# A two-layer attention kernel: unread TensorE passes in the last second layer, ten small loads on another queue, units and jobs at other slots

## The chip, the cores and the metric

The kernel runs on 1 core of one Trainium2 chip. The metric is the device time of one execution, in microseconds (us); lower is better. The kernel before takes 3834.04 us, the median of 3 runs (3832.09 to 3839.49). The profiled execution is another one and took 3831.53 us.

## The reference, cut to what matters

For 64 sequences of 128 rows and 160 columns, and a context of 77 rows of 256 each:

```python
# layer 0, 20 heads of 64
n = layer_norm(x);  x = x + attention(n, n)          # self attention
n = layer_norm(x);  x = x + attention(n, context)    # cross attention
x = geglu_ff(layer_norm(x)) + x                      # 160 -> 2*640 -> 160
# layer 1, 20 heads of 8; 73 text rows and 4 image rows of the context
probs_t = softmax(q @ k_t * scale);  text = probs_t @ v_t
qsem = l2norm(probs_t @ text_ehs)                    # per head
fused = q @ k_ip * scale + 0.5 * (qsem @ l2norm(ip_ehs))
image = (softmax(fused) * spatial_mask) @ v_ip
out = (text + image) @ W_out + b_out + x
```

All of it is in 32-bit floats.

## The kernel before, in words

Four sequences make a group; there are 16 groups. One list of **slots** sets the order of everything: `STEP` is 60 slots to a group, and slot numbers run on, so the last group's first layer ends at slot 959 and its second layer lies behind it. In each slot at most one **unit** begins: in layer 0 (`"l0"`) one pair of heads of two sequences, 40 units to a group; in layer 1 (`"l1"`) four heads of one sequence, 20 units to a group. The second layer of group g is worked off between the first-layer units of group g+1: `L1_SLOT` lists its 20 slots, the first-layer units take those left. The last group's second layer has no first layer beside it; `LAST_L1_SLOT` lists its slots, 964 to 973 and 980 to 989.

Every engine walks through the slots in its own loop and does what each slot holds in a fixed order, so each engine's instructions are a fixed list, and only semaphores tie the engines together. A unit goes through five steps: scores on TensorE into a bank `PS` (`scores`, one slot ahead), maximum on VectorE (`softmax_in`), exponentials on ScalarE (`exp`), transposes on TensorE into `PT` (`probs_transposed`, a slot later), product with the values into a bank `PV` (`probs_v`, two slots later). For a first-layer unit VectorE also sums and GpSimd normalises (`prob_sums`, `normalise`), and `wo` adds its part of the output into the bank `PW`. For a second-layer unit VectorE does six instructions on the result, three slots after the unit's own (`unit_out`).

The other work is a **job** at a slot of its own: `qk`, `kc`, `v` (projections of a unit), `xT` (transposes after a layer norm), `ff` and `down`, `q1` and `k1` (second-layer queries and keys), `vip`, `ctx1` (per sequence b: Gram matrix and values of the context, copied into `gv`), and the tail of each sequence b of the second layer: `ipT`, `ip`, `oT1`, `y`. Jobs take the two banks `PG` in turn: a job waits until the last but one job's bank has been read. A layer norm (g, k, h), with h the half of the group, has its slot in `NORM_SLOT`; k = 0 to 2 are those of layer 0, k = 3 only copies rows.

Second-layer queries and keys reach their places by DMA, from SyncE's queue: three transfers for each of five parts w, `q1st` for each half and `k1st` for each group. GpSimd forms `kbd` from `k1st`.

Ahead of the loops stands a setup block (lines 242 to 310), which ends for all engines together. In it SyncE starts the loads of the first x and of the weights of keys, queries and values, ScalarE those of twelve small rows (`EARLY`: six of the layer norms, four biases, `b_1` and `fside`; `b_1` is read with 4 bytes to a piece). Then `SPLITS` are worked off at `SPLIT_SLOT`: each weight is split into a high part (ScalarE, `split_high`) and a low part (VectorE, `split_low`). The first group begins at slot -15, its first unit is at slot 20.

Of the kernel before, what the change touches and what calls it, by code (L numbers as in the profile page):

```python
# [5 lines left out]
def xattn_program(nc: bass.Bass, D, out: bass.AP):  # L6
# [13 lines left out]
    GROUPS = B // GB  # L20
    NP = H // 2
    HB = GB // 2
    HT = HB * 128
# [14 lines left out]
    F = FF // 128  # L38
# [4 lines left out]
    STEP = 60  # L43
    L1_SLOT = [6, 7, 9, 10, 11, 13, 14, 15, 17, 18, 22, 26, 27, 29, 33, 37, 41, 45, 49, 53]
    LAST_L1_SLOT = list(range(4, 14)) + list(range(20, 30))
    L0_SLOT = [s for s in range(STEP) if s not in L1_SLOT]
    NORM_SLOT = {(0, 0): -12, (0, 1): -2, (1, 0): 25, (1, 1): 40, (2, 0): 52, (2, 1): 65, (3, 0): 60, (3, 1): 71}
    FF_SLOT = [56, 56, 56, 56, 56, 68, 68, 68, 68, 68]
# [3 lines left out]

    SPLIT_SLOT = [8, 9, 17, 18, 28, 30, 31, 31, 32, 32, 49, 50]
    SPLIT_LOAD = [None, None, None, None, 21, 28, 21, 21, 21, 21, 47, 47]
    RAW_LOAD = {"kc": 22, "vc": 34}
    KEYS_ZERO = 32
    LEAD = {"q": 2, "kc": 1, "vc": 1}
    PLAIN_SLOT = 48

    FIRST_L0_SLOT = list(range(STEP - NL0, STEP))  # L60
    FIRST_NORM_SLOT = {(0, 0): 8, (0, 1): 22, (1, 0): 33, (1, 1): 43, (2, 0): 53}
    VIP_SLOT = 58
    K1_SLOT = (52, 58)

    PT_LAG, PV_LAG, OUT_LAG = 1, 2, 3
    CTX1_SLOT = {0: 59, 1: 65, 2: 82, 3: 89}
    LAST_CTX1_SLOT = {0: 58, 1: 65, 2: 80, 3: 85}

    ctx = ExitStack()
    with ctx:  # L70
# [171 lines left out]
        with nc.Block() as block:  # L242
            @block.sync
            def _(sp):
                sp.dma_start(xres[:, 0, :, :], x_dram[0:HB].rearrange("b n c -> n b c")).then_inc(x_first, 16)
                for i in range(2):
                    for src, p0, p1 in SPLITS[i][0]:
                        sp.dma_start(SPLITS[i][3][p0:p1], src).then_inc(split_in[i], 16)
                w = D["L0_xattn_a1_wq"]
                sp.dma_start(q_raw[:, 0, :], w[0:128, :]).then_inc(raw_in["q"], 16)  # L250
                for src, p0, p1 in rest_of(w):
                    sp.dma_start(q_raw[p0:p1, 1, :], src).then_inc(raw_in["q"], 16)
                for i in range(2, 4):
                    for src, p0, p1 in SPLITS[i][0]:
                        sp.dma_start(SPLITS[i][3][p0:p1], src).then_inc(split_in[i], 16)

            @block.scalar
            def _(act):

                for i, (dst, src) in enumerate(EARLY):  # L260
                    act.dma_start(dst, src, allow_slow_non_contiguous=True).then_inc(ln_in if i < 2 else early_in, 16)

# [102 lines left out]
        def slots(at):  # L365
            table = {}
            for t, what in at:
                table.setdefault(t, []).append(what)
            return lambda t: table.get(t, [])
# [3 lines left out]

        NORMS = sorted((STEP * g + (s if g else FIRST_NORM_SLOT.get((k, h), s)), g, k, h)
                       for g in range(GROUPS) for (k, h), s in NORM_SLOT.items())
        NORM = {x[1:]: i for i, x in enumerate(NORMS)}
# [12 lines left out]
        def ctx1_slot(g, b):  # L389
            return STEP * g + (CTX1_SLOT if g < GROUPS - 1 else LAST_CTX1_SLOT)[b]  # L390

        stacks_at = slots([(STEP * g + Q1_SLOT[h] + 1 + w, ("q1", g, h, w))
                           for g in range(GROUPS) for h in range(2) for w in range(W1)]
# [4 lines left out]
            + [(t + (1 if k == 3 else 2), ("xT", g, k, h)) for t, g, k, h in NORMS]  # L398
            + [(STEP * g + Q1_SLOT[h], ("q1", g, h)) for g in range(GROUPS) for h in range(2)]
            + [(STEP * g + PREP_SLOT[h] + 1, ("cT", g, h)) for g in range(GROUPS) for h in range(2)]  # L400
            + [(tail_slot(g, b) + d, (kind, g, b)) for d, kind in ((5, "ipT"), (6, "ip"), (7, "oT1"), (8, "y"))
               for g in range(GROUPS) for b in range(GB)]
            + [(STEP * g + FF_SLOT[F * h + F - 1] + 1, ("down", g, h)) for g in range(GROUPS) for h in range(2)]
            + [(STEP * g + s, ("ff", g, i)) for g in range(GROUPS) for i, s in enumerate(FF_SLOT)]
            + [(STEP * g + K1_SLOT[r], ("k1", g, r)) for g in range(GROUPS) for r in range(2)]
# [87 lines left out]
        with nc.Block() as block:  # L493
# [7 lines left out]
            def _(sp):  # L501
# [53 lines left out]
                def load_raw(kind):  # L555
                    sp.wait_ge(S["split_done"], 4 if kind == "kc" else 10)
                    w = D["L0_xattn_a2_wk" if kind == "kc" else "L0_xattn_a2_wv"]
                    for c, raw in enumerate(kc_raw if kind == "kc" else vc_raw):
                        sp.dma_start(raw, w[128 * c:128 * c + 128, :]).then_inc(raw_in[kind], 16)

                for t in range(FIRST, LAST):
                    for kind, i in stores_at(t):
                        store_slice(kind, i)
# [46 lines left out]
            def _(pe):  # L610
# [27 lines left out]
                def ctx_rows(ps, w, c0, n, b, rows):  # L638

                    for c in range(2):  # L640
                        for i, (hw, hc) in enumerate(SPLIT3):
                            last = mm(ps, cT[:, c, hc, TS * b:TS * b + rows], w[:, c, hw, c0:c0 + n],  # L642
                                      start=(c == 0 and i == 0), stop=(c == 1 and i == 2))
                    return last

                def slice_in(name):
# [197 lines left out]

                for t in range(FIRST, LAST):
                    if t + 1 in UNIT_AT:
                        scores(UNIT_AT[t + 1])
# [591 lines left out]
```

## Time and profile before

| | before |
|---|---|
| time, median of 3 runs | 3834.04 us |
| profiled execution | 3831.53 us |
| its span | 3829.7 us |
| TensorE busy (matmul) | 3622.5 us, 95% |
| VectorE busy | 2563.7 us, 67% |
| ScalarE busy | 2584.0 us, 67% |
| GpSimd busy | 1335.9 us, 35% |
| data moved by DMA | 313.38 MB, mean 82 GB/s |

The span runs from the first to the last instruction that the profiler saw; what lies around it is 1.8 us. Times in rows are counted from the span's start. The busy share of TensorE is an upper limit, since the ends of its pipelined matmuls are modelled. Its clock has two levels, 1.2 and 2.4 GHz; the granted clock is given as a share of the higher.

### The profile page before, as it was taken

To read this page: it belongs to the slowest core of one execution; us is meant where nothing else is said; L and a number is where in the kernel's file an instruction comes from. 1 tells how busy PE (TensorE), PEld (TensorE's weight loads), DVE (VectorE), ACT (ScalarE), POOL (GpSimd) and SP (SyncE) were. 2 spreads that over 40 slices of the span, in tenths; PEclk is the share of its full clock that TensorE was granted. 3 is DMA by queue.
4 is the path that set the end of the run, shared out by engine and by line. 5 is a ranking of instruction groups with operands and counts; after the bars stand their busy time and mean duration, and the time that the engine had idled before them with its cause. 6 is when DMAs were issued, how large, how long until landed. Compare 5 with 4: busy or idle time off the path is not lost. (4 is left out here: it accounts for less than half of the span.)

```text
span 3829.7 us, 88852 instructions
## 1 busy us (share of the span) xinstructions
PE 3622.5 (95%) x29632; PEld 3341.0 (87%) x29632; DVE 2563.7 (67%) x8159; ACT 2584.0 (67%) x8021; POOL 1335.9 (35%) x1658
## 2 busy tenths in 40 slices
PE   5999999999999999999999999999999999999988
PEld 5888989889898898989989898898988989899877
DVE  6667676676766767676676766767667676766755
ACT  5666676766767667676676767667676676766654
POOL 2233343333433334343333433334333343433323
PEclk9999999999999999999999999999999999999986
DMA  5522313223141322313223142231323223132220
GB/s 160 168 65 75 101 46 118 60 86 89 45 121 55 97 78 59 113 47 108 66 77 99 46 121 56 86 89 45 120 56 96 78 58 114 48 108 64 76 67 12
DMA packets 210716, 313.38 MB, mean 82 GB/s; under 512 B 31232, under 2 KB 167520, under 8 KB 210272
## 3 DMA queue, kind: packets, MB, share of 16 engines
q1 hardware_dynamic: 207392, 306.87, 27.2%
q8 instruction: 250, 4.10, 0.5%
q10 hardware_dynamic: 2880, 0.83, 0.1%
q14 instruction: 194, 1.59, 0.1%
HBM read 267.97 MB, written 14.42 MB: 74 GB/s over the span
## 5 line engine op out<-in xcount | busy, mean ns | idle before, releaser
L1376 POOL TENSOR_TENSOR SE<-SE,rs 128x512 f32<-128x512 f32 (+1 forms) x640 | 556.5, 870 | 1792.2 <-DVE rs L1210 1792.2
L961 ACT ACTIVATE SE<-PS,mx 128x128 f32<-128x128 f32 (+2 forms) x3840 | 979.0, 345 | 255.1 <-DVE qq L1234 109.1
L816 PE MATMUL PT<-ident,SE 128*128 128x128 f32 (+2 forms) x3840 | 585.9, 276 | 36.2 <-POOL SE L1376 35.3
L947 ACT ACTIVATE PTs<-PT 128x512 f32<-128x512 f32 (+2 forms) x960 | 574.7, 599 | 58.1 <-PE PT L816 38.7
L1205 DVE TENSOR_REDUCE sums<-SE 128x4 f32<-128x512 f32 (+1 forms) x640 | 366.8, 573 | 341.1 <-ACT SE L961 338.8
L1194 DVE TENSOR_REDUCE mx<-PS 128x4 f32<-128x512 f32 (+2 forms) x960 | 505.0, 526 | 59.4 <-PE PS L794 42.3
L816 PEld LDWEIGHTS PT<-ident,SE 128*128 128x128 f32 (+2 forms) x3840 | 469.9, 145 | 63.7 <-POOL SE L1376 49.6
L1368 POOL TENSOR_TENSOR n<-qq,p_half 128x4 f32<-128x4 f32 x320 | 323.0, 1009 | 469.1 <-DVE qq L1234 469.0
L774 PE MATMUL PW<-w_o,OTs 128*128 128x160 f32 x2560 | 417.0, 300 | 1.0 <-ACT OTs L939 1.0
L794 PE MATMUL PS<-qk 128*128 128x256 f32 x1280 | 348.9, 395 | 47.5 <-ACT qk L887 47.5
L884 ACT ACTIVATE qk<-PG 128x256 f32<-128x256 f32 x640 | 252.2, 394 | 196.1 <-PE PG L620 192.2
L830 PE MATMUL PV<-PTs,v_sb 128*64 128x128 f32 (+1 forms) x5120 | 370.9, 281 | 0.0
L774 PEld LDWEIGHTS PW<-w_o,OTs 128*128 128x128 f32 x2560 | 362.2, 191 | 1.4 <-ACT OTs L939 1.4
L840 PE MATMUL PV<-gv,PTs 73*128 73x86 f32 x2560 | 335.2, 275 | 0.7 <-DVE SE L1232 0.7
L830 PEld LDWEIGHTS PV<-PTs,v_sb 128*64 128x64 f32 (+1 forms) x5120 | 271.8, 137 | 67.2 <-issue 55.6
L840 PEld LDWEIGHTS PV<-gv,PTs 73*128 73x128 f32 x2560 | 325.1, 197 | 0.9 <-issue 0.8
L794 PEld LDWEIGHTS PS<-qk 128*128 128x128 f32 x1280 | 219.6, 191 | 101.5 <-issue 80.1
L617 PE MATMUL PG<-nT,q_slice 128*128 128x256 f32 x640 | 247.7, 387 | 28.2 <-DVE cipT L1108 10.6
L642 PE MATMUL PG<-vc_slice,cT 128*77 128x256 f32 x1920 | 265.5, 287 | 0.2 <-DVE nT L1115 0.2
L939 ACT ACTIVATE OTs<-PV 128x256 f32<-128x256 f32 x640 | 223.8, 381 | 57.0 <-PE PV L830 54.5
L1130 DVE COPY v_sb<-PG 128x512 f32<-128x512 f32 (+1 forms) x320 | 218.1, 682 | 57.5 <-PE PG L642 54.6
L887 ACT ACTIVATE qk<-PG 64x256 f32<-64x256 f32 x640 | 240.5, 376 | 3.7
(205 smaller groups left out, 7853.5 us busy)
## 6 DMA issues: line engine op xcount, KB each, us to landing
q_slice<-q_split SPq DMA_DIRECT2D x630, 192.0 KB, 2.5
vc_slice<-vc_split SPq DMA_DIRECT2D x155, 512.0 KB, 3.6
kc_slice<-kc_split SPq DMA_DIRECT2D x150, 256.0 KB, 2.7
q1st<-q_hi SPq DMA_DIRECT2D x320, 32.0 KB, 1.9
k1st<-k_hi SPq DMA_DIRECT2D x160, 38.5 KB, 1.9
xres<-in_x_dram SPq DMA_DIRECT2D x32, 160.0 KB, 2.3
q1st<-q_lo SPq DMA_DIRECT2D x160, 32.0 KB, 1.9
out_dram<-x SPq DMA_DIRECT2D x64, 80.0 KB, 1.6
```

Source lines behind the costliest of these rows:

```text
L642: last = mm(ps, cT[:, c, hc, TS * b:TS * b + rows], w[:, c, hw, c0:c0 + n], start=(c == 0 and i == 0), stop=(c == 1 and i == 2))
L774: last = mm(PW[:, C * b:C * b + C], OTs[:, n % 2, 128 * b:128 * b + 128], w_o[n // U0][:, p, :], start=(p == 0 and b == 0), stop=(p == NP ...
L794: last = mm(ps[:, 2 * J * b:2 * J * b + 2 * J], qk[:, n % 2, 0, 128 * b:128 * b + 128], keys[:, :, J * b:J * b + J], start=True, stop=True)
L816: last = tr(PT[0:J, 128 * i:128 * i + 128], SE[:, place % 4, J * i:J * i + J], ident[:, :])
L830: last = mm(PV[DH * e:DH * e + DH, 128 * b:128 * b + 128], v_sb[0:J, n // 2 % 2, b, 2 * (n % 2) + e, :], PTs[0:J, place % 3, 128 * i:128 * ...
L840: last = mm(PV[:, GV * i + off:GV * i + off + GS + D1], PTs[0:TT, place % 3, 128 * i:128 * i + 128], gv[:, b % 2, 2 * w + i // 2, off:off ...
L947: a_(PTs[0:J, place % 3, :], PT[0:J, :], ACT.Copy).then_inc(S["pts_done"], 1)
L961: last = a_(SE[:, place % 4, J * i:J * i + J], PS[place % 2][:, step * i:step * i + J], ACT.Exp, bias=mx[:, place % 2, i:i + 1])
L1194: v.tensor_reduce(mx[:, place % 2, :], sc[:, :, 0:J], AX, ALU.max, negate=True).then_inc(S["mx_done"], 1)
L1205: v.tensor_reduce(sums[:, n % 2, :], SE[:, place % 4, 0:4 * J].rearrange("p (i j) -> p i j", j=J), AX, ALU.add)\
L1368: gp.tensor_tensor(n20[:, b % 2, 4 * w:4 * w + 4], qq[:, b % 2, 4 * w:4 * w + 4], p_half[:, 0:4], ALU.pow)\
L1376: gp.tensor_tensor(e, e, rs[:, n % 2, :].unsqueeze(2).to_broadcast([128, 4, J]), ALU.mult)\
```

## The change

1. In the setup block ScalarE starts only the first two small loads. The other ten are started by SyncE at slot 10 (`EARLY_SLOT`). The five loads of the value weights move out of the setup block to the head of SyncE's loop. The split of `w_k0_rem` moves from slot 9 to 16.
2. Second-layer units 15 and 16 of every group but the last move from slots 37 and 41 to 36 and 38; five first-layer units move by a slot. `K1_SLOT` begins at 53 where it was 52.
3. For the last group alone: norm (2,1) from 65 to 63, (3,0) from 60 to 58, (3,1) from 71 to 69; the second half of `ff` from 68 to 67; `q1` from 62 and 73 to 61 and 72; `ctx1` from 58, 65, 85 to 59, 64, 84.
4. `keep_busy` is new: TensorE multiplies 128 x 128 by 128 x 256 of `nT` into `PW`, whose result nobody reads; 20 times ahead of the first scores of the last second layer, and 14 times ahead of each of its four `ipT`. That is 76 passes.

```diff
-    L1_SLOT = [6, 7, 9, 10, 11, 13, 14, 15, 17, 18, 22, 26, 27, 29, 33, 37, 41, 45, 49, 53]
+    L1_SLOT = [6, 7, 9, 10, 11, 13, 14, 15, 17, 18, 22, 26, 27, 29, 33, 36, 38, 45, 49, 53]
-    SPLIT_SLOT = [8, 9, 17, 18, 28, 30, 31, 31, 32, 32, 49, 50]
+    SPLIT_SLOT = [8, 16, 17, 18, 28, 30, 31, 31, 32, 32, 49, 50]
+    EARLY_SLOT = 10
...
-    LAST_CTX1_SLOT = {0: 58, 1: 65, 2: 80, 3: 85}
+    KEEP_BUSY = STEP * GROUPS + LAST_L1_SLOT[0] - 1
+    LAST_NORM_SLOT = {(2, 0): 52, (2, 1): 63, (3, 0): 58, (3, 1): 69}
+    LAST_FF_SLOT = [56, 56, 56, 56, 56, 67, 67, 67, 67, 67]
+    LAST_Q1_SLOT = [61, 72]
+    LAST_CTX1_SLOT = {0: 59, 1: 64, 2: 80, 3: 84}
...
-                for i in range(2, 4):
-                    for src, p0, p1 in SPLITS[i][0]:
-                        sp.dma_start(SPLITS[i][3][p0:p1], src).then_inc(split_in[i], 16)
...
-                for i, (dst, src) in enumerate(EARLY):
-                    act.dma_start(dst, src, allow_slow_non_contiguous=True).then_inc(ln_in if i < 2 else early_in, 16)
+                for dst, src in EARLY[0:2]:
+                    act.dma_start(dst, src, allow_slow_non_contiguous=True).then_inc(ln_in, 16)
...
+                for i in range(2, 4):
+                    for src, p0, p1 in SPLITS[i][0]:
+                        sp.dma_start(SPLITS[i][3][p0:p1], src).then_inc(split_in[i], 16)
                 for t in range(FIRST, LAST):
+                    if t == EARLY_SLOT:
+                        for dst, src in EARLY[2:]:
+                            sp.dma_start(dst, src, allow_slow_non_contiguous=True).then_inc(early_in, 16)
...
+                def keep_busy(n):
+                    pe.wait_ge(S["x_done"], 4 * GROUPS)
+                    for _ in range(n):
+                        mm(PW[:, 0:HT], nT[:, 0, 0, 0:128], nT[:, 0, 0, :], start=True, stop=True)
...
                 for t in range(FIRST, LAST):
+                    if t == KEEP_BUSY:
+                        keep_busy(20)
                     if t + 1 in UNIT_AT:
                         scores(UNIT_AT[t + 1])
...
                     for name in late_at(t):
+                        if name[0] == "ipT" and name[1] == GROUPS - 1:
+                            keep_busy(14)
```

SyncE's list at the start of the program, before (`SE`, `plain`, `kx1` and `later` hold raw weights; the branch at L242 is the end of the setup block):

```order
L245 DMA xres<-in_x_dram 128x2x160
L248 DMA SE<-in_L0_xattn_a1_wk_dram 128x1280
...
L252 DMA kx1<-in_L0_xattn_a1_wq_dram 32x1280 x4
L255 DMA later<-in_L0_xattn_a1_wv_dram 128x1280
L255 DMA later<-in_L0_xattn_a1_wv_dram 32x1280 x4
L242 UNCONDITIONAL_BRANCH
...
L573 DMA w_o0<-in_L0_xattn_a1_wo_dram 128x10x160
L519 DMA xres<-in_x_dram 128x2x160
...
L541 DMA q_split<-q_slice 128x384 x5
```

The same place after the change (the branch at L247 ends the setup block):

```order
L257 DMA kx1<-in_L0_xattn_a1_wq_dram 32x1280 x4
L247 UNCONDITIONAL_BRANCH
...
L574 DMA later<-in_L0_xattn_a1_wv_dram 32x1280 x4
L590 DMA w_o0<-in_L0_xattn_a1_wo_dram 128x10x160
L530 DMA xres<-in_x_dram 128x2x160
...
L578 DMA ln_g<-in_L0_xattn_ln2_g_dram 128x160
...
L578 DMA b_1<-in_L0_xattn_ff_b1_dram 128x10x1
L578 DMA fside<-in_fside_S_0_dram 128x1
L530 DMA xres<-in_x_dram 128x2x160
L552 DMA q_split<-q_slice 128x384 x5
```

The value weights now stand behind the end of the setup block, and the ten small loads behind them and ahead of the first stores of `q_split`.

VectorE's list in a middle group from slot 40 on, before (from the maximum of unit `l1` 16 on; `rr` to `qq` are `unit_out` of `l1` 15, `st6` the next layer norm):

```order
L1194 TENSOR_REDUCE mx<-PS1 128x4
L1199 COPY sip<-PS1 128x16
L1220 RECIPROCAL rr<-PV1 128x4
...
L1234 TENSOR_REDUCE qq<-SE 128x4
L1125 COPY kx1<-PG1 64x154 x2
L1130 COPY v_sb<-PG0 77x512
L1052 BN_STATS st6<-xres 128x6 x2
...
L1194 TENSOR_REDUCE mx<-PS0 128x4
L1125 COPY kx1<-PG0 64x154 x2
L1070 SCALAR_TENSOR_TENSOR nx<-lt,rstd,ln_b 128x128
```

The same place after the change (`rr` to `qq` are now `unit_out` of `l1` 16):

```order
L1222 TENSOR_REDUCE mx<-PS1 128x4
L1153 COPY kx1<-PG1 64x154 x2
L1080 BN_STATS st6<-xres 128x6 x2
...
L1233 TENSOR_REDUCE sums<-SE 128x4
L1238 RECIPROCAL rs<-sums 128x4
L1222 TENSOR_REDUCE mx<-PS0 128x4
L1248 RECIPROCAL rr<-PV0 128x4
...
L1262 TENSOR_REDUCE qq<-SE 128x4
L1153 COPY kx1<-PG1 64x154 x2
L1158 COPY v_sb<-PG0 77x512
L1098 SCALAR_TENSOR_TENSOR nx<-lt,rstd,ln_b 128x128
```

A `unit_out` that stood ahead of the norm's statistics has gone to the slot before, and the next one has come from slot 44 to 41, between the statistics and the norm's output.

TensorE's list at the end of the last first layer, before (from `vip` on):

```order
L734 MATMUL PG0<-plain,cipT 16x160 x2
L739 MATMUL PG1<-cT 73x82 x6
...
L744 MATMUL PG1<-vip_sb,pick 80x160
L816 MATMUL PT<-ident,SE 77x128 x4
...
L678 MATMUL PG0<-ident,nx 128x128 x4
L774 MATMUL PW<-w_o1,OTs 128x160 x4
L617 MATMUL PG1<-nT,w_q1h_hi 128x256
...
L620 MATMUL PG1<-nT,w_q1h_rem 128x256
L802 MATMUL PS0<-kbd,q1st 128x308
L747 MATMUL PG0<-ident,sip 80x128
```

And after the change:

```order
L758 MATMUL PG0<-plain,cipT 16x160 x2
L840 MATMUL PT<-ident,SE 77x128 x4
...
L702 MATMUL PG1<-ident,nx 128x128 x4
L763 MATMUL PG0<-cT 73x82 x6
...
L637 MATMUL PG1<-nT,w_q1h_rem 128x256
L798 MATMUL PW<-w_o1,OTs 128x160 x4
L668 MATMUL PW<-nT 128x256 x20
L826 MATMUL PS0<-kbd,q1st 128x308
L771 MATMUL PG0<-ident,sip 80x128
```

`ctx1` has gone behind the unit's transposes and products, `xT` and `q1` have come ahead of the last `wo`, and the 20 unread passes stand between that `wo` and the first scores.

## Rows read from the trace of the kernel before

**Rows 1.** Page: granted TensorE clock in 40 slices, in tenths

```profile
PEclk9999999999999999999999999999999999999986
```

**Rows 2.** Timeline of the setup: start us, length us, engine, line, what, idle before it

```profile
8.83 4.00 SPq L255 DMA_DIRECT2D later<-in_L_xattn_a_wv_dram  x5
9.76 9.45 ACTq L261 DMA_DIRECT2D fside<-in_fside_S_dram  x1
19.62 1.28 ACT L978 ACT_TABLE_LOAD   x1 [19.62 <-PEq L242]
```

**Rows 3.** Timeline of the first layer's start, same columns

```profile
24.80 3.56 DVE L1265 TENSOR_TENSOR w_k_rem<-plain,w_k_rem 32x1280 fp32r<-32x1280 f32 x2
...
25.40 1.60 POOL L1360 TENSOR_TENSOR xres<-xres,bias 128x320 f32<-128x320 f32 x1 [3.52 <-DMA fside<-in_fside_S_dram]
25.97 0.60 ACT L880 ACTIVATE nT<-PG 128x512 fp32r<-128x512 f32 x1 [2.62 <-PE PG L678]
...
30.32 0.55 PE L617 MATMUL PG<-nT,q_slice 128*128 128x256 f32 x1 [4.38 <-DVE q_slice L1277]
...
40.96 1.04 POOL L1376 TENSOR_TENSOR SE<-SE,rs 128x512 f32<-128x512 f32 x1 [13.96 <-DVE rs L1210]
```

**Rows 4.** Timeline of group 5 at slot 45, one of fifteen alike

```profile
1323.86 0.17 DVE L1220 RECIPROCAL rr<-PV 128x4 f32<-128x4 f32 x1
...
1324.81 0.46 DVE L1234 TENSOR_REDUCE qq<-SE 128x4 f32<-128x292 f32 x1
...
1325.87 0.39 PE L617 MATMUL PG<-nT,q_slice 128*128 128x256 f32 x1 [0.56 <-DVE kx L1125]
```

**Rows 5.** Windows of the last stretch: busy us (count) of each engine, then the granted clock

```profile
3711.00:3714.00 3.00, 2.00 (x12) 1.83 (x12) 2.49 (x8) 1.04 (x3) 2.10 (x3) 0.85 0.24 60
...
3759.00:3762.00 3.00, 2.42 (x21) 2.20 (x20) 2.89 (x15) 1.71 (x6) 1.21 (x2) 1.00 0.00 0
3783.00:3786.00 3.00, 3.00 (x15) 3.00 (x14) 2.30 (x11) 2.77 (x12) 0.70 (x1) 0.50 0.01 3
```

**Rows 6.** What TensorE waited for after 3700 us: total, times, longest

```profile
PE PG L747 <- DVE sip L1296: 9.1, 3, 3.9
...
PE PT L816 <- POOL SE L1376: 2.0, 1, 2.0
...
PE PW L774 <- ACT OTs L939: 1.0, 1, 1.0
```

**Rows 7.** Timeline where the last second layer starts, by engine

```profile
3723.10 0.69 DVE L1157 SCALAR_TENSOR_TENSOR q_lo<-PG,q_hi 128x512 fp32r<-128x512 f32 x1 [1.92 <-ACT q_hi L911]
...
3727.59 0.54 SPq L590 DMA_DIRECT2D q1st<-q_hi  x1
...
3726.97 0.59 PE L802 MATMUL PS<-kbd,q1st 96*128 96x308 f32 x1 [4.61 <-issue]
...
3730.78 0.60 PE L802 MATMUL PS<-kbd,q1st 96*128 96x308 f32 x1 [3.01 <-issue]
```

**Rows 8.** Chain that ended last: pieces on TensorE, at either clock

```profile
3720.86 0.21 PE PG L618
...
3754.35 0.44 PE PT L816 x4
3754.79 0.86 PE PV L840 x8
...
3790.79 0.26 PE PS L802
3791.05 0.85 PE PT L816 x4
3791.90 1.64 PE PV L840 x8
```

**Rows 9.** VectorE's timeline where it works without a gap

```profile
3758.86 0.45 DVE L1194 TENSOR_REDUCE mx<-PS 128x4 f32<-128x292 f32 x1
...
3760.63 0.45 DVE L1194 TENSOR_REDUCE mx<-PS 128x4 f32<-128x292 f32 x1
```

More of the change, by code:

```diff
@@ L43, in xattn_program @@
     STEP = 60
-    L1_SLOT = [6, 7, 9, 10, 11, 13, 14, 15, 17, 18, 22, 26, 27, 29, 33, 37, 41, 45, 49, 53]
-    LAST_L1_SLOT = list(range(4, 14)) + list(range(20, 30))
+    L1_SLOT = [6, 7, 9, 10, 11, 13, 14, 15, 17, 18, 22, 26, 27, 29, 33, 36, 38, 45, 49, 53]
+    LAST_L1_SLOT = [4, 5, 6, 7, 8, 9, 10, 11, 12, 13, 20, 21, 22, 23, 24, 25, 26, 27, 28, 29]
     L0_SLOT = [s for s in range(STEP) if s not in L1_SLOT]
@@ L62, in xattn_program @@
     VIP_SLOT = 58
-    K1_SLOT = (52, 58)
+    K1_SLOT = (53, 58)
     PT_LAG, PV_LAG, OUT_LAG = 1, 2, 3
     CTX1_SLOT = {0: 59, 1: 65, 2: 82, 3: 89}
-    LAST_CTX1_SLOT = {0: 58, 1: 65, 2: 80, 3: 85}
+    KEEP_BUSY = STEP * GROUPS + LAST_L1_SLOT[0] - 1
[3 more added lines that the diff above has]
+    LAST_CTX1_SLOT = {0: 59, 1: 64, 2: 80, 3: 84}
     ctx = ExitStack()
@@ L372, in xattn_program, with norm_slot, ff_slot, q1_slot @@
         outputs_at = slots((product_slot(UNIT_AT[t]) + OUT_LAG - PV_LAG, UNIT_AT[t]) for t in sorted(UNIT_AT))
-        NORMS = sorted((STEP * g + (s if g else FIRST_NORM_SLOT.get((k, h), s)), g, k, h)
-                       for g in range(GROUPS) for (k, h), s in NORM_SLOT.items())
+        def norm_slot(g, k, h):
+            own = FIRST_NORM_SLOT if g == 0 else LAST_NORM_SLOT if g == GROUPS - 1 else {}
+            return STEP * g + own.get((k, h), NORM_SLOT[(k, h)])
+        def ff_slot(g):
+            return FF_SLOT if g < GROUPS - 1 else LAST_FF_SLOT
+        def q1_slot(g):
+            return Q1_SLOT if g < GROUPS - 1 else LAST_Q1_SLOT
+        NORMS = sorted((norm_slot(g, k, h), g, k, h) for g in range(GROUPS) for k, h in NORM_SLOT)
         NORM = {x[1:]: i for i, x in enumerate(NORMS)}
@@ L390, in ctx1_slot @@
             return STEP * g + (CTX1_SLOT if g < GROUPS - 1 else LAST_CTX1_SLOT)[b]
-        stacks_at = slots([(STEP * g + Q1_SLOT[h] + 1 + w, ("q1", g, h, w))
+        stacks_at = slots([(STEP * g + q1_slot(g)[h] + 1 + w, ("q1", g, h, w))
                            for g in range(GROUPS) for h in range(2) for w in range(W1)]
@@ L398, in xattn_program @@
             + [(t + (1 if k == 3 else 2), ("xT", g, k, h)) for t, g, k, h in NORMS]
-            + [(STEP * g + Q1_SLOT[h], ("q1", g, h)) for g in range(GROUPS) for h in range(2)]
+            + [(STEP * g + q1_slot(g)[h], ("q1", g, h)) for g in range(GROUPS) for h in range(2)]
             + [(STEP * g + PREP_SLOT[h] + 1, ("cT", g, h)) for g in range(GROUPS) for h in range(2)]
@@ L402, in xattn_program @@
                for g in range(GROUPS) for b in range(GB)]
-            + [(STEP * g + FF_SLOT[F * h + F - 1] + 1, ("down", g, h)) for g in range(GROUPS) for h in range(2)]
-            + [(STEP * g + s, ("ff", g, i)) for g in range(GROUPS) for i, s in enumerate(FF_SLOT)]
+            + [(STEP * g + ff_slot(g)[F * h + F - 1] + 1, ("down", g, h)) for g in range(GROUPS) for h in range(2)]
+            + [(STEP * g + s, ("ff", g, i)) for g in range(GROUPS) for i, s in enumerate(ff_slot(g))]
             + [(STEP * g + K1_SLOT[r], ("k1", g, r)) for g in range(GROUPS) for r in range(2)]
```

## The prediction

> **What bounds the kernel now.** I read the page first. The granted clock [rows 1] is full nearly to the end and falls in the last two slices; TensorE is the only engine that is busy nearly throughout. So three places matter: the start, where it has no work yet; the fifteen middle groups, where a gain counts only if it removes a wait of TensorE; and the last second layer, where the clock is low.
>
> The timeline of the setup shows the start. SyncE has issued the query weights by 8.83 us and the value weights by 12.83, but the setup block ends at 19.6, because ScalarE's last small load holds its queue from 9.76 to 19.21 [rows 2]. Then a chain runs: layer norm, transposes, remainder split of `w_k0`, `nT`, `q_slice`, and the first projection at 30.32 [rows 3].
>
> A middle group, read by its timeline, has one TensorE wait that the moved units touch: 0.56 us at slot 45, where `qk` waits for a bank that VectorE's `kx` has not yet read, because a `unit_out` stands ahead of it [rows 4]. That `unit_out` lasts from 1323.86 to 1325.27, 1.41 us.
>
> The windows of the end show the clock falling at about 3713.1 (0.85 in that window of 3 us is 0.9 us at half), after TensorE had been busy for 2.00 of 3 us. It is full again for a time, at 2.42 busy of 3, and it is at half from 3783 on although TensorE is busy for 3.00 of 3 us with transposes and products of units [rows 5]. One unit's transposes and products then take 0.85 + 1.64 us against 0.44 + 0.86 at the full clock, and with its scores 2.75 [rows 8]. VectorE, without a gap, takes 1.77 us for a second-layer unit [rows 9]. So at 1.2 GHz TensorE sets the pace of this layer, and at 2.4 GHz VectorE does.
>
> **The change part by part.** The sum is made against the profiled execution, 3831.53 us; the median of the runs stands 2.5 above it, and I add the sum to the median.
>
> *Setup.* Without ScalarE's ten loads the block should end with SyncE's last issue, at 8.8, plus the same 0.4 us: 9.2 instead of 19.6, 10.4 earlier. Against that, the remainder split of 3.56 us has moved behind `nT`. It began at 24.80, and `nT` could have begun when ScalarE was done at 26.57 [rows 3]; the 1.8 us between were covered by the split and are a hole of VectorE now. 10.4 - 1.8 = 8.6, from which I take 0.6 for weights that land late: -8.0. The other end is a stall on SyncE's queue: its five value loads take 4.0 us, 0.8 each; four more loads and nine small ones at the same 0.8 would end at about 23.6; if `fside` then holds the queue for 9.45 us again, it is 33.1. Behind it stand the stores of `q_split`, which free the three `q_slice` buffers, and GpSimd's first normalisation stands behind `bias`, which waits for the same loads (they landed 15.6 us after `fside` was issued, at 25.40 [rows 3]; here at 39). Without the stall that normalisation is due at 40.96 - 8 = 33, so it would come about 6 us late: -2.
>
> *Units 15 and 16.* Work is unchanged. The 0.56 us goes, since no `unit_out` stands in slot 44 any longer. But VectorE now has `unit_out` of 15 at slot 39 and of 16 at 41, with the norm's statistics between them, and `kx` of slot 41 stands behind both, where TensorE's `qk` of slot 42 waits for its bank. By the listed order and the durations of this stretch VectorE comes there about half a us after TensorE. So a wait of 0.5 takes the place of 0.56: with a tenth for a smaller wait that goes too, 15 x -0.16 = -2.4. Bounds: the new wait is nothing, 15 x -0.66 = -9.9; or it is a whole `unit_out`, 15 x (1.41 - 0.56) = +12.7. `k1` a slot later is costed at nothing: TensorE has other work on both sides.
>
> *The last group up to the first second-layer scores.* `ctx1` no longer stands ahead of the last unit's exponentials, so the wait of 2.0 for GpSimd goes, and with `xT` and `q1` ahead of the last `wo` the wait of 1.0 for ScalarE [rows 6]. Then the clock need not fall at 3713.1: of the 9.2 us to the last pass of `q1` at 3722.36, 8.2 are busy and take half at 2.4 GHz, -4.1. The last `wo` is behind `q1` now: -0.5. Together -7.6, and the wait of 4.61 for `q1st` [rows 7] stays. Into it go the 20 unread passes. At 0.21 each at 1.2 GHz [rows 8] that is 4.2, at half of it 2.1; they start after the last `x` of VectorE, about 1 us after `q1` ends, so 2.1 is hidden and 4.2 would be late by about 0.6. Bounds: -3.5 (the clock falls as before) and -7.6.
>
> *From the first scores to the second half.* Part 1 of `q1st` stands behind a triple of `k1st`, as before, and part 2 now too: `q_lo` ends at 3723.79 and part 1 is issued at 3727.59, two triples later, 1.9 each [rows 7]. Against that `ctx1` of b = 1 goes into the wait, and `ff` is a slot earlier, which puts the dense passes ahead of a unit at the low clock (2.75 against 1.77, 1.0). I take -1, with 0 and -5 as bounds.
>
> *The 56 passes at the four `ipT`.* Three `ipT` have waited for VectorE's `sip`, 9.1 us in all, the longest 3.9 [rows 6]; there 14 passes take 2.9 or 1.5 us and are mostly hidden. The second stands in the middle of units with TensorE fully busy and costs 2.9 at 1.2 GHz. If the clock rises with it, each of the last eight units saves 2.75 - 1.77 = 0.98. I take half of this and the passes at half way between their prices: -3.9 + 2.2, and for jobs between the units -0.8: -2.5. Bounds: -7.3 (all eight, 1.5 for the passes, -1 for the jobs) and +2.9. In the last chain the two tails have their steps at half clock; if they run at the full one I count -2.6, if not, the passes that do not fit their gap cost +1.4. I take -1.
>
> Sum: -8.0 - 2.4 - 7.6 - 1 - 2.5 - 1 = **-22.5**: 3809.0 for the profiled execution, 3811.5 for the median.
>
> **The rivals.** *The clock holds.* If the dense passes keep the full clock through the last second layer, the four `ipT` parts give -7.3 and -2.6 instead of -2.5 and -1, and the first five units and `ff` some 3 us more: 9.4 more, 3802. Rows 5 speak against: TensorE busy 2.42 of 3 us was followed by a fall before 3783, and a share like it is what VectorE's pace leaves (0.44 + 0.86 of 1.77 us, and the scores). On what lets the clock fall, the Trainium skill, "TensorE: Matmul & The Clock Gate", section "Why this matters for your kernels", says that drops in mid-kernel are avoided by leaving no long idle gaps between matmul bursts. By that rule the clock would stay up between the second `ipT` and the end, and the time is this rival's, 3802. The trace does not bear it out, as the clock was at half with 3.00 of 3 us busy.
>
> *The start's gain is lost on SyncE's queue*: -2 instead of -8, 3817.5. For it speaks the 9.45 us of `fside`; against it that this was while all the first weights moved, and less is in flight at 24 us. The Trainium skill, "DMA: Bandwidth & Descriptors", section "Queues, rings and completion order", says that a DMA engine takes one queue's descriptors in order and takes turns between queues. By that rule the ten small loads, which had turns of their own on ScalarE's queue, now stand behind all the weights; the time is this rival's, 3817.5. No run shows it yet.
>
> *The passes don't do what they are for*: the clock is as before and they only cost: +2.9 and +1.4 instead of -2.5 and -1, 0 instead of -1, 8.8 more: 3820.
>
> *VectorE falls behind in every group.* Two `unit_out` within three slots delay the jobs behind them. If the new wait is one `unit_out`, the middle costs +12.7 and the sum is -7.4: 3826.6. If both are late, 2.8 us against 0.56, it costs 15 x 2.24 = +33.6, and the sum is +13.5: 3847.5, slower. It decides from a new wait of 1.9 us on (15 x 1.34 = 20.1, the rest of the sum). For it: VectorE is at work nearly without a gap there; against it: before, an even denser stretch of slots 40 and 41 was without a wait.
>
> **How the numbers follow.** Forecast 0.44, clock holds 0.18, start lost 0.15, passes only cost 0.09, one `unit_out` late 0.08, two late 0.06. A measurement of this kernel can tell some 0.2%, 7.7 us. Faster: the first four, 0.86; same: 0.08; slower: 0.06. The predicted time is the forecast's, 3811.5, rounded to 3811. Its own range, by the bounds of start and middle, is 3803 to 3822; the range reaches to the clock's rival with a middle wait gone (3802 - 7.5) and to one late `unit_out`: 3794 to 3826.
>
> **What would show it.** Setup block ends near 9.2, first projection near 22.3, the first `rs` of VectorE 8 us earlier. In a middle group no wait at slot 45 and one of about 0.5 at slot 42, the group 0 to 0.3 us shorter. First second-layer scores 7.6 us earlier against the last group's start, the clock full up to them, then half for some 10 us. Full clock after each block of 14, but not to the end. I am wrong if a group's length changes by over 0.5 us, if small loads land after the first normalisation is due, or if the clock holds.

## The result and the profile after

The changed kernel takes 3804.03 us, the median of 4 runs (3800.84 to 3805.68), where the kernel before takes 3834.81 in the same measurement (3832.09 to 3839.49). The ratio is 0.9928, 95% interval 0.9915 to 0.9941: 0.72% faster, some 28 us. The two medians of this measurement are 30.8 us apart; in the four later sets of runs the kernel before has medians of 3830.95 to 3832.64, which fits the 28. The forecast was 3811, the range 3794 to 3826. The profiled execution is the fastest of the four, 3800.84; its span is 3799.1, so the differences of the two traces below come to 30.6 us.

The page, in answer to [rows 1]:

```profile
PEclk9999999999999999999999999999999999999998
```

Windows of the last group cut at three scores of its second layer: start of the group to the first scores, to the eleventh, to the twentieth, to the end. Columns as in [rows 5]; the granted clock is the third number from the right. The kernel before:

```profile
3480.18:3726.97 246.79, 230.07 (x1878) 211.48 (x1877) 158.05 (x504) 161.40 (x501) 83.24 (x102) 0.97 0.23 66
3726.97:3777.95 50.98, 40.74 (x230) 38.41 (x231) 30.44 (x122) 22.96 (x66) 18.38 (x23) 0.67 0.07 18
3777.95:3805.79 27.84, 27.59 (x130) 26.02 (x131) 15.81 (x68) 14.01 (x47) 9.90 (x13) 0.51 0.06 15
3805.79:3829.71 23.92, 12.32 (x65) 9.14 (x64) 12.83 (x59) 5.18 (x17) 6.04 (x6) 0.63 0.03 8
```

And the changed kernel:

```profile
3470.55:3709.95 239.40, 229.10 (x1897) 210.77 (x1897) 156.78 (x504) 161.92 (x501) 84.48 (x102) 1.00 0.23 67
3709.95:3753.88 43.93, 34.27 (x246) 32.17 (x245) 29.69 (x122) 23.03 (x66) 18.37 (x23) 0.88 0.10 25
3753.88:3776.46 22.58, 21.11 (x144) 18.91 (x145) 15.35 (x67) 13.58 (x47) 9.91 (x13) 0.85 0.05 13
3776.46:3799.09 22.63, 14.29 (x91) 12.26 (x91) 13.07 (x60) 5.31 (x17) 6.05 (x6) 0.87 0.03 8
```

The four stretches are 7.4, 7.1, 5.3 and 1.3 us shorter. With the start (group 1 begins at 221.48 where it began at 226.14, 4.7) and fourteen groups that together take 3249.07 us and took 3254.04 (5.0), that is the whole difference. The prediction had 7.6, then 4.5 for the last three together (measured 13.6), 8.0 for the start and 2.4 for the groups. So what was new to explain is the gain behind the first scores, and whether the unread passes bring it. These are differences of two single executions; the experiments show that some 9 us of them lie with an early fall of the clock, which the kernel before has in some executions only, and some 4 with a stretch that no other execution repeats.

Timeline of the start, in answer to [rows 2] and [rows 3]:

```profile
8.71 1.28 ACT L1006 ACT_TABLE_LOAD   x1 [8.71 <-PEq L247]
...
11.44 8.83 SPq L530 DMA_DIRECT2D xres<-in_x_dram  x1
...
19.82 0.42 ACT L1019 ACTIVATE q_slice<-kx 128x256 fp32r<-128x256 f32 x1 [3.39 <-DMA kx<-in_L_xattn_a_wq_dram]
...
21.43 2.98 DVE L1293 TENSOR_TENSOR w_k_rem<-plain,w_k_rem 32x1280 fp32r<-32x1280 f32 x2 [0.27 <-ACT w_k_rem L1006]
...
24.66 0.55 PE L634 MATMUL PG<-nT,q_slice 128*128 128x256 f32 x1 [8.87 <-DVE w_k_rem L1293]
...
32.05 1.07 POOL L1388 TENSOR_TENSOR xres<-xres,bias 128x320 f32<-128x320 f32 x1 [21.08 <-DMA fside<-in_fside_S_dram]
...
35.68 1.04 POOL L1404 TENSOR_TENSOR SE<-SE,rs 128x512 f32<-128x512 f32 x1 [2.56 <-DVE rs L1238]
```

The setup block ends at 8.7, 10.9 us earlier, a little better than the 9.2 that was forecast. But the first projection comes at 24.66, only 5.7 earlier: ScalarE waits 3.39 us for the query weights to land, `w_k_rem` follows behind, and TensorE waits for it. The stall of 9.45 us that ScalarE's queue had is now one of 8.83 us on SyncE's queue, on the load of `xres`. The small loads land at 32.05. GpSimd then adds `bias`, is done at 33.12, and waits 2.56 us more: its first normalisation begins at 35.68 (40.96 before), released by VectorE's `rs`, not by `bias`.

A middle group, in answer to [rows 4]; first the kernel before at slots 52 and 53, which the prediction did not look at:

```profile
1352.05 0.42 ACT L918 ACTIVATE k_hi<-PG 128x292 fp32r<-128x292 f32 x1 [1.45 <-PE PG L730]
...
1353.50 0.43 ACT L884 ACTIVATE qk<-PG 128x256 f32<-128x256 f32 x1
...
1354.16 0.56 PEld L794 LDWEIGHTS PS<-kx,qk 128*128 128x128 f32 x4 [0.30 <-issue]
```

The changed kernel in the same places:

```profile
1346.27 1.19 PE L651 MATMUL PG<-cT,w_k1h 128*128 128x328 f32 x6
1346.38 0.40 ACT L912 ACTIVATE qk<-PG 128x256 f32<-128x256 f32 x1
...
1347.65 0.51 PE L818 MATMUL PS<-kx,qk 128*128 128x154 f32 x2
```

Before, `k1` was projected ahead of the unit's `qk`; its two copies `k_hi` stood ahead of the exponentials on ScalarE, `qk` was copied at 1353.50, and TensorE's scores waited 0.30 us for it. Now `k1` is projected while ScalarE copies `qk`. Slots 52 and 53 take 5.18 us where they took 5.52. The stretch of the moved units, slots 34 to 45, takes 44.53 and took 44.61.

### The profile page after: what moved, and what is told of

Same layout as the page of the kernel before. It is cut to its first block, busy times and chain, and to the rows that moved or that the text cites. A ratio compares the mean times of both kernels' runs of the same rounds, so it can differ in the third digit from the quotient of the medians.

```text
span 3799.1 us, 88944 instructions
## 1 busy us (share of the span) xinstructions
PE 3608.9 (95%) x29708; PEld 3328.8 (88%) x29708; DVE 2547.7 (67%) x8159; ACT 2592.4 (68%) x8021; POOL 1352.4 (36%) x1658
## 4 chain that ended last, share of the span: by engine, by line
PE 60%; DVE 17%; ACT 11%; issue 8%; POOL 4%; DMA 1%; SPq 0%; ACTq 0%; DVEq 0%; POOLq 0%
PE PS L818 8%; PE PT L840 6%; PE PV L854 6%; PE PW L798 5%; PE PG L659 5%; ACT SE L989 4%; PE PG L651 4%; PE PG L634 4%; PE PV L864 3%; DVE sums L1233 3%; PE PG L637 3%; PE PG L635 3%; PE PG L636 3%; POOL SE L1404 3%; PE PG L742 2%
## 5 line engine op out<-in xcount | busy, mean ns | idle before, releaser
L1396 POOL TENSOR_TENSOR n<-qq,p_half 128x4 f32<-128x4 f32 x320 | 345.3, 1079 | 490.2 <-DVE qq L1262 490.1
L864 PEld LDWEIGHTS PV<-gv,PTs 73*128 73x128 f32 x2560 | 317.5, 192 | 1.2 <-issue 1.1
```

The lines of the kernel that those rows point to most:

```text
L864: last = mm(PV[:, GV * i + off:GV * i + off + GS + D1], PTs[0:TT, place % 3, 128 * i:128 * i + 128], gv[:, b % 2, 2 * w + i // 2, off:off ...
```

## The experiments

Every median is compared with runs of the kernel before on the same chip; its medians there were 3831.09 (e1 to e4), 3830.95 (e5 to e8), 3831.41 (e9 to e11) and 3832.64 (e12). Its single runs lie between 3824.8 and 3841.2, those of the changed kernel within 5 us.

**Passes: e1 to e4.** e1 is the changed kernel without both `keep_busy`:

```diff
-                    if t == KEEP_BUSY:
-                        keep_busy(20)
-                        if name[0] == "ipT" and name[1] == GROUPS - 1:
-                            keep_busy(14)
```

> The changed kernel without any of the 76 unread passes; everything else as changed. Clock theory (the passes keep TensorE at 2.4 GHz through the last second layer, and that gives some 10 us of the last group's 20): about 3814 us, and the granted clock is at half for most of the last 85 us. Order theory (the moved jobs of the last group give those 20 us, and the clock follows from the denser order by itself): 3803 to 3806, with the clock mostly full. If the passes only cost, it is faster than 3804.

e2 is the kernel before with these lines added and nothing else.

> The kernel before with the 76 passes and nothing else of the change. Clock theory: the last group gains some 10 us, 3834 becomes about 3824. Order theory: the passes need the moved jobs or only cost: 3834 to 3840. The 20 passes ahead of the first scores stand in a wait of 4.6 us and should cost nothing by either.

e3 keeps the 20 and leaves out the 14, e4 the other way round.

> The changed kernel with the 20 passes ahead of the first scores, without the 56 at the four ipT. Clock theory in the form that the blocks of 14 do it: as without any passes, about 3814. In the form that the 20 hold the clock over the wait for the first keys and queries: 3804 to 3808.

> The changed kernel with the 56 passes at the four ipT, without the 20. If the blocks of 14 carry the gain: 3804 to 3806. If the 20 carry it: about 3812. The trace should show at which block the clock rises.

| kernel | median us | ratio to before, interval |
|---|---|---|
| e1, no passes | 3809.56 | 0.9944 (0.9930 to 0.9957) |
| e2, passes alone | 3832.10 | 1.0001 (0.9992 to 1.0010) |
| e3, the 20 only | 3804.48 | 0.9929 (0.9917 to 0.9942) |
| e4, the 14s only | 3808.72 | 0.9944 (0.9931 to 0.9956) |

All passes together are worth 5 us, all of it comes from the 20, and on the kernel before they give nothing. The 5 us do not rest on runs of different chips: e3's five runs (3803.01 to 3806.47) all lie below e1's five (3808.01 to 3813.73), and both kernels ran on one. e3 came out as its second expectation had it; e1, e2 and e4 lie between the two times that each had named. The last three windows of e3, to set beside those of the changed kernel, show where the 56 go:

```profile
3709.88:3757.97 48.09, 36.54 (x232) 34.44 (x231) 29.84 (x122) 23.02 (x66) 18.38 (x23) 0.77 0.09 23
3757.97:3778.79 20.82, 19.69 (x130) 17.54 (x131) 15.25 (x67) 13.81 (x47) 9.92 (x13) 0.80 0.05 14
3778.79:3802.69 23.90, 12.29 (x63) 9.13 (x63) 13.06 (x60) 5.20 (x17) 6.05 (x6) 0.67 0.03 8
```

In the third stretch the 14 raise the clock from 0.80 to 0.85 and make it 1.76 us longer; in the fourth they raise it from 0.67 to 0.87 and make it 1.27 shorter. e4 against e1 repeats it (22.28 against 20.63 us, then 23.04 against 24.57). Adding them to the kernel before, e2:

```profile
3728.84:3778.66 49.82, 40.84 (x244) 38.47 (x245) 30.44 (x122) 22.92 (x66) 18.40 (x23) 0.73 0.08 19
3778.66:3804.29 25.63, 23.82 (x144) 21.95 (x145) 15.63 (x68) 13.49 (x47) 9.91 (x13) 0.73 0.05 14
3804.29:3830.36 26.07, 20.57 (x91) 18.37 (x91) 13.10 (x59) 5.35 (x17) 6.05 (x6) 0.57 0.02 7
```

Against the trace of the kernel before this is 2.2 us won and 2.2 lost. Against e7's, shown below, whose last group has the same code without passes and whose clock also falls late, it is 3.6 and 0.7 us lost. The passes do raise the mean clock; they take at least the time that it saves.

**Units, k1 and the start: e5 to e8.** e5 and e6 are the kernel before with one table changed each:

```diff
-    L1_SLOT = [6, 7, 9, 10, 11, 13, 14, 15, 17, 18, 22, 26, 27, 29, 33, 37, 41, 45, 49, 53]
+    L1_SLOT = [6, 7, 9, 10, 11, 13, 14, 15, 17, 18, 22, 26, 27, 29, 33, 36, 38, 45, 49, 53]
```

> The kernel before with units 15 and 16 at slots 36 and 38, nothing else. Theory from the two traces (slots 34 to 45 of a group take 44.61 us before and 44.53 after, so the move gives 0.08 us a group): -1 us, 3833. Rival (the move gives the 0.36 us a group that middle groups have become shorter): -5, 3829.

```diff
-    K1_SLOT = (52, 58)
+    K1_SLOT = (53, 58)
```

> The kernel before with the first k1 at slot 53 where it was 52, nothing else. Theory from the two traces (slots 52 and 53 take 5.52 us before and 5.18 after): -0.34 us in each of 16 groups, -5 us, 3829. Rival: nothing, 3834.

e7 is the kernel before with the change of the setup block alone (value weights and ten small loads in SyncE's loop, `w_k_rem` at 16).

> The kernel before with the setup edit alone: ten small loads on the other queue at slot 10, value weights behind the setup block, split of w_k0_rem at slot 16. The traces show the first scores 5.6 us earlier and the first full group 4.7 us earlier: -5 us, 3829. Rival (the last group's start alone decides and the gain is taken up by a later wait): -1 or less.

e8 is the changed kernel with the split of `w_k_rem` back at slot 9:

```diff
-    SPLIT_SLOT = [8, 16, 17, 18, 28, 30, 31, 31, 32, 32, 49, 50]
+    SPLIT_SLOT = [8, 9, 17, 18, 28, 30, 31, 31, 32, 32, 49, 50]
```

> The changed kernel with the split of w_k0_rem back at slot 9. In the changed kernel VectorE has nothing from 17.4 to 20.3 us, waiting for the query weights, and does this split of 3 us behind them. Hole theory: the split fills that hole and the first projection comes 3 us earlier: 3801. Rival (the weights' landing sets the start, the value weights at 23.1 us): the first scores come earlier, but VectorE waits for the value weights and the group ends at the same time: 3804.

| kernel | median us | ratio to before, interval | in its trace |
|---|---|---|---|
| e5, units | 3829.14 | 0.9996 (0.9986 to 1.0005) | a middle group 232.15 us (before 232.3) |
| e6, k1 | 3826.23 | 0.9989 (0.9979 to 1.0000) | a middle group 232.06 |
| e7, setup | 3823.53 | 0.9978 (0.9968 to 0.9988) | first scores at 27.82 (before 33.48) |
| e8, split at 9 | 3803.05 | 0.9928 (0.9916 to 0.9940) | first scores at 24.04 (changed kernel 27.84) |

e6's group is 0.26 us shorter, some 3.6 in fourteen, and e5's 0.15 us, 2.1; the changed kernel has 0.36. The medians hardly separate either from nothing (e6's interval ends at 1), the traces do. e7 gives 0.22%, 5 to 12 us by its interval, where some 5 were expected. e8, at 3803.05, lies between its two expectations and can't be told from the changed kernel. It shows that a second thing binds the start. Timeline of its first, third and fourth scores:

```profile
24.04 2.08 PE L818 MATMUL PS<-qk 128*128 128x256 f32 x4 [1.52 <-ACT qk L915]
...
32.15 0.42 ACT L1019 ACTIVATE q_slice<-kx 128x256 fp32r<-128x256 f32 x1 [3.35 <-DMA q_split<-q_slice]
...
34.79 2.04 PE L818 MATMUL PS<-qk 128*128 128x256 f32 x4 [2.92 <-ACT qk L915]
...
39.46 1.10 PE L818 MATMUL PS<-qk 128*128 128x256 f32 x4 [0.78 <-ACT qk L915]
```

The first scores gain 3.8 us, the third (36.04 in the changed kernel) only 1.3: ScalarE waits 3.35 us for a store of `q_split`, which SyncE issues behind the small loads, and TensorE waits 2.92 for ScalarE. The fourth come at 39.46, where the changed kernel has them at 39.30, but that last loss is the clock's: this trace is of e8's slowest execution (3810.38), and from 33 to 39 us its granted clock is 0.72 and 0.71, where the changed kernel's is 1.00. So the queue of the prediction's second rival is at work, but it takes some two thirds of what a better split order would give, and nothing of what the change gave.

**The last group's slots: e9 and e10.** e9 is the kernel before with these tables alone; e10 is the changed kernel without them:

```diff
-    LAST_NORM_SLOT = {(2, 0): 52, (2, 1): 63, (3, 0): 58, (3, 1): 69}
-    LAST_FF_SLOT = [56, 56, 56, 56, 56, 67, 67, 67, 67, 67]
-    LAST_Q1_SLOT = [61, 72]
-    LAST_CTX1_SLOT = {0: 59, 1: 64, 2: 80, 3: 84}
+    LAST_NORM_SLOT = {}
+    LAST_FF_SLOT = FF_SLOT
+    LAST_Q1_SLOT = Q1_SLOT
+    LAST_CTX1_SLOT = {0: 58, 1: 65, 2: 80, 3: 85}
```

> The kernel before with one part of the change: the slots of the last group (norms, second half of ff, q1, ctx1); no passes, setup and units as before. Theory A (the prediction's terms for the last group hold: the order itself gives 7.6 us up to the first second-layer scores, and 1 behind them): 8.6 us less than before, some 3822, and first scores 7 us earlier against the last group's start than in the run of the kernel before (there 246.8 us). Theory B (the order gives little by itself, and most of the gain is that the clock falls late, which in some executions of the kernel before it does anyway, with scores at 243): first scores at 239 to 240, time 3824 to 3828. Theory C (order and clock only pay together with the passes): no change, 3830.

> The changed kernel with the last group's slots put back as before, the 76 passes kept. Theory A (order gives 7.6 to 8.6): 3812. Theory B (the order gives some 4, passes and order are worth little alone): 3808 to 3811, first scores of the last second layer at 243 us after the group's start. Theory C (order and passes pay only together): 3814 to 3818, the sum of setup, k1 and units alone.

e9: 3824.88 us, ratio 0.9982 (0.9971 to 0.9993), 0.18% or 7 us, as its second expectation had it. e10: 3820.11, ratio 0.9962 (0.9948 to 0.9977), so with the passes there the slots are worth 13 to 16 us, where the largest expectation, 3818, had 14.

The ratios fit together. Units, `k1`, setup and slots, each put alone on the kernel before (e5, e6, e7, e9), give 0.04, 0.11, 0.22 and 0.18%, together 0.55%; with all four and no pass, e1, it is 0.56%. With the new slots taken out and the passes left in, e10, it is 0.38%, what units, `k1` and setup give by themselves (0.37%): passes with the old slots are worth nothing, as in e2. With the new slots they bring the changed kernel from 0.56 to 0.72%, 6 us. By these numbers the slots work without the passes, and the passes only with the slots. Each ratio is uncertain by 0.1%.

e9's windows; the trace is of its second fastest execution (3820.18):

```profile
3484.49:3723.54 239.05, 226.63 (x1878) 208.38 (x1877) 158.04 (x504) 161.63 (x501) 83.59 (x102) 1.00 0.23 67
3723.54:3773.66 50.12, 38.26 (x230) 35.55 (x231) 30.01 (x122) 23.02 (x66) 18.37 (x23) 0.71 0.09 23
3773.66:3794.55 20.89, 19.75 (x130) 17.60 (x131) 15.25 (x67) 13.70 (x47) 9.91 (x13) 0.80 0.05 14
3794.55:3818.44 23.89, 12.28 (x63) 9.12 (x63) 13.05 (x60) 5.20 (x17) 6.05 (x6) 0.67 0.03 8
```

Without a single pass the first scores come at 239.1 us after the group's start, where the kernel before has 246.8, and the clock is at 0.80 in the third stretch where it was at 0.51. That is not the slots' doing alone, though. In the profiled execution of the kernel before the clock falls 232.9 us after the group's start, and in e5's at 232.8; in those of e7 and e6, whose last group is the same code, at 240.9 and 240.4, and the first scores then come at 243. e7's windows:

```profile
3480.64:3723.77 243.13, 226.37 (x1878) 208.29 (x1877) 157.98 (x504) 161.84 (x501) 83.42 (x102) 1.00 0.23 67
3723.77:3773.78 50.01, 38.35 (x230) 35.91 (x231) 30.41 (x122) 22.92 (x66) 18.39 (x23) 0.70 0.08 19
3773.78:3795.82 22.04, 19.93 (x131) 17.93 (x131) 15.62 (x68) 13.87 (x47) 9.91 (x13) 0.79 0.06 16
3795.82:3821.21 25.39, 15.68 (x63) 12.70 (x63) 13.08 (x59) 5.19 (x17) 6.04 (x6) 0.52 0.02 7
```

The same code takes 349.4 to 349.5 us from the group's start to the end when the clock falls early and 340.1 to 340.6 when it falls late: 3.7 us up to the first scores and 5.3 behind them. So of the 15.6 us between e9 (333.95) and the kernel before (349.53) some 9 are the early fall and 6 to 7 are left. e9's median shows 7, with an interval of 3 to 11.

The fall was early, 230.6 to 232.9 us after the group's start, in three of the six traces with the old slots (e10, e5, the kernel before) and late, 240.4 to 243.9, in the other three (e6, e7, e2). In the eight with the new slots it was never early: 237.2 (e1), 239.6 (e9) and 241.6 us (e4) without the 20 passes, 244.2 to 268.5 with them. e2, with passes and old slots, had it at 243.9 and e10, with the same two, at 230.6, and there the passes come only after the fall: passes do not decide whether it is early.

**More cover at the first scores: e11 and e12.** e11 issues the last two triples of `k1st` ahead of the second half's `q1st`:

```diff
-                          + [(STEP * g + K1_SLOT[1] + 1 + w, ("k1", g, 1, w)) for g in range(GROUPS) for w in range(W1)])
+                          + [(STEP * g + K1_SLOT[1] + 1 + (w if g < GROUPS - 1 else min(w, 2)), ("k1", g, 1, w))
+                             for g in range(GROUPS) for w in range(W1)])
```

> The changed kernel, but in the last group SyncE issues the last two triples of k1st ahead of the first q1st of the second queries' half instead of between them. The keys are ready long before. Theory A (SyncE's queue sets the first scores of the last second layer): each further q1st is issued 1.9 us earlier than the one before it, the second scores come 1.9 us earlier, the third 3.8, TensorE's waits there shrink by about 3 us, the time falls by 2 to 4 us to some 3800 to 3802. Theory B (the clock and VectorE's pace set the end of this stretch): scores come earlier, but the end does not, 3803 to 3805.

3806.03 us, ratio 0.9933 (0.9919 to 0.9948): nothing gained, in kind as its second expectation had it (3803 to 3805). The third scores do come earlier, at 3714.76 where the changed kernel has 3716.91, but then TensorE waits for VectorE:

```profile
3717.65 0.63 PE L703 MATMUL PG<-ident,nx 128*128 128x128 f32 x4 [2.08 <-DVE nx L1101]
```

That wait is not in the changed kernel. The order of transfers was not the only thing behind these scores.

e12 leaves out the 14s and puts passes into TensorE's two waits there:

```diff
-                    if t == KEEP_BUSY:
-                        keep_busy(20)
+                    if t in (KEEP_BUSY, KEEP_BUSY + 1, KEEP_BUSY + 2):
+                        keep_busy({KEEP_BUSY: 20, KEEP_BUSY + 1: 16, KEEP_BUSY + 2: 12}[t])
```

> The changed kernel without the 14 passes at each ipT, and with 16 more passes ahead of the second and 12 ahead of the third scores of the last second layer, where TensorE waits 2.6 and 2.0 us. In the kernel with the 20 passes alone the clock fell 244.7 us after the last group's start and was full again at 254.9. Theory A (the clock falls because TensorE does little in these two waits): it holds until after the dense passes of the feed-forward, past 260 us, the eleventh scores come at 283 or earlier and the median is 3800 to 3802. Theory B (what the passes cover makes no difference here): the clock falls at 244 to 248 as before and the median is that of the 20 alone, 3803 to 3806.

3808.00 us, ratio 0.9934 (0.9920 to 0.9949), no better than e3's 0.9929 and above both expected times. Its windows, from its fastest execution (3803.67):

```profile
3724.00:3737.00 13.00, 12.49 (x99) 11.75 (x98) 7.61 (x32) 8.15 (x22) 4.08 (x5) 1.00 0.00 1
3737.00:3740.00 3.00, 1.06 (x5) 1.06 (x6) 2.16 (x8) 1.79 (x6) 3.00 (x5) 0.79 0.03 5
3740.00:3743.00 3.00, 3.00 (x15) 2.99 (x15) 1.98 (x11) 1.56 (x5) 1.44 (x2) 0.50 0.00 0
3743.00:3746.00 3.00, 3.00 (x16) 3.00 (x15) 1.19 (x6) 0.59 (x1) 1.01 (x1) 0.50 0.00 0
...
3749.00:3752.00 3.00, 3.00 (x16) 3.00 (x16) 2.79 (x15) 0.59 (x1) 1.66 (x2) 0.50 0.22 54
```

The first half of what was expected happened: the clock held through the feed-forward, to 268.5 us after the group's start, where e3 lost it at 244.7. The second half did not: it then fell and stayed at half for 27 us; e3's longest such stretch has 16. The eleventh scores came at 286.5 us after the group's start, e3's at 287.5. What was held early was lost later.

## Why the prediction was right, and where its sizes were off

**Part by part, by the ratios of the runs.** Forecast against measured: setup 8.0 against 8; units and `k1` 2.4 against 6; the last group's slots 8.6 (7.6, and 1 behind the first scores) against 7; passes 3.5, all from the 14s, against 6, all from the 20. The sum was 22.5 and is 28. The right time is in part luck: two parts were too small, the passes worked in another place than forecast, and the forecast started from one execution with an early fall.

**The last group up to the first scores**: 7.6 forecast, 7.4 measured between the two traces. The forecast was 3.5 for waits and order and 4.1 for a clock that need not fall. The second part is there, but it is no property of the kernel before: e6 and e7, with its last group, have the first scores at 242.8 and 243.1 us, 3.7 earlier than its trace. The order gives the other 3.7 (239.4), and e9 (239.1) and e1 (238.6) show that it does so without passes. The wait of 2.0 for GpSimd is 0.41 now; the wait for ScalarE's `OTs` stayed (0.96 again), a part of this term that did not come. The window of 3711 to 3714 in [rows 5], read as what came before the fall, holds the fall itself; in the 3 us ahead of it TensorE was busy for 1.02:

```profile
3710.00:3713.00 3.00, 1.02 (x10) 1.00 (x9) 2.83 (x13) 1.48 (x5) 1.10 (x2) 1.00 0.22 56
```

The 20 passes took 2.65 us at the full clock and ended as the first scores began. The forecast had them at nothing, and they are the only passes that count.

**The start**: 8.0 forecast, 4.7 in the traces, 5 to 12 by e7's ratio. In the traces the step that was too small is "0.6 for weights that land late": ScalarE alone waits 3.39 us for the query weights. Moving the split of `w_k_rem` was costed as a hole of 1.8; it cost 3.8 at the first scores and 1.3 at the third (e8). The rival of the small loads did not come about: they landed in time. The Trainium skill, "DMA: Bandwidth & Descriptors", section "Queues, rings and completion order", has a queue's descriptors taken in order; the trace agrees in so far as the small loads, issued from 21.23 on behind the weights, landed at 32.05, but what depends on them was due later.

**The middle**: 2.4 forecast, 5.0 measured. The moved units gave 0.08 to 0.15 us a group, where 0.16 was forecast: a wait of 0.3 for `kx` and one of 0.2 for `v_sb` stand in place of the 0.56. The failed step is "`k1` a slot later is costed at nothing: TensorE has other work on both sides". It gave 0.26 to 0.34 us a group, since it had stood ahead of a unit's `qk` on ScalarE. The row had no engine's name, only 0.30 of issue on the weight load.

**From the first scores on**: 4.5 forecast, 13.6 in the traces. By the time this is the rival in which the clock holds (13.9 for the same three terms); by its mechanism it is not. The clock did not hold, it was at half for 22.9 us of this stretch, in five falls, and the 14 passes, by which it was to hold, are worth nothing: 2.5 and 1 forecast, nothing measured, as e1 with e4 and e3 with the whole change show. Their term assumed that a unit saves the 0.98 us between TensorE's and VectorE's pace; the third stretch shows a saving smaller than the passes' own time. What made the 13.6 is where the falls of the clock lie. From the first scores to the eleventh the length goes with the granted clock whatever the kernel: 52.1 us at 0.66 (e1), 51.0 at 0.67, 50.0 at 0.70 (e7), 48.1 at 0.77 (e3), 47.0 at 0.81 (e12), 43.9 at 0.88. The 43.9 is one execution's luck: e8 and e11, with the 20 and the 14s too, take 48.1 and 47.5. Nor is it the first 14 passes: they begin at 3749.18, and by the tenth scores (3741.19, e3 3743.07) the changed kernel was already 1.9 us ahead of e3 with the same instructions. So some 4 of the 13.6 belong to the one profiled execution, as its 3800.84 against the median of 3804.03 says, and 5.3 to the early fall in the kernel before. What is left, some 4.3, is close to the 4.5 of the forecast, but it comes with the 20 passes and not with the 14s: behind the first scores e7 takes 97.4 us, with the new slots e1 97.3, e9 94.9 and e4 97.5, and with the 20 as well e3 92.8.

The Trainium skill, "TensorE: Matmul & The Clock Gate", section "Why this matters for your kernels", has drops in mid-kernel avoided by leaving no long idle gaps. The trace agrees in one place: with the two waits filled the clock held for 24 us more (e12), and it fell in a window in which TensorE was busy for 1.06 of 3 us. Elsewhere it does not. In e12 the clock then stayed at half through four windows on end with TensorE busy for 3.00 of 3 us, and in e10 it fell, at 3699.3, with no wait of TensorE over 0.6 us in the 10 us before:

```profile
3690.00:3693.00 3.00, 3.00 (x26) 3.00 (x24) 1.28 (x4) 0.59 (x1) 0.70 (x1) 1.00 0.00 0
3693.00:3696.00 3.00, 2.42 (x24) 1.96 (x22) 0.76 (x3) 0.49 (x2) 0.00 (x0) 1.00 0.00 0
3696.00:3699.00 3.00, 2.18 (x24) 1.50 (x22) 1.36 (x7) 2.40 (x9) 0.00 (x0) 1.00 0.26 65
3699.00:3702.00 3.00, 1.83 (x8) 1.83 (x9) 2.62 (x9) 1.01 (x4) 1.94 (x3) 0.55 0.24 58
```

The measurement decides: filling the two gaps moved the fall and did not remove it.

**Open**: what decides in which executions the kernel before loses the clock early was not found; nor why the falls come where they come when the engine is busy. That the new slots keep the early fall away is read from one trace of each kernel, none of eight against three of six; why they do is not shown. Nor is it shown how the 20 passes, in the same wait in e2 and e10, come to be worth 6 us with the new slots and nothing with the old. A kernel with only these two parts was not run.

## What to carry to other kernels

Unread passes can raise the clock and still not pay. Here 20 in one wait paid with one order of jobs and not with another, 28 more in two further waits did not (e12), and 56 between units took what they saved: price them against what the following work saves at the full clock, and run the kernel without them. A job that is moved is never free by default: look at what it stands ahead of on the engine that copies its bank, and read the short waits that the profile puts down to issue. When executions of one kernel differ by 15 us, compare several traces before explaining a stretch by the change.

## What the runs showed of the hardware

TensorE's clock was at half for 27 us on end, with the engine busy for 23.8 of them (e12), and it fell with no wait of the engine over 0.6 us in the 10 us before (e10). The last group's same code lost it at 232.9 or at 240.9 us after the group's start in different executions, worth 9 us at the end. Short falls also lie in some of the otherwise equal middle groups, which then take 1.1 to 1.4 us more (232.31 and 233.65 in the kernel before, 231.95 and 233.07 in the changed one). A single load of `xres` held SyncE's queue for 8.83 us while the weights issued ahead of it were in flight, as `fside` had held ScalarE's for 9.45: it is not a property of the small load. That it goes with the traffic is the likeliest reading; no run isolates it.
